# LayerNorm statistics summed over feature tiles on VectorE before the ones-matmul, and a cast moved to ScalarE

## The reference

```python
x = x + cumsum_1024(layernorm(x) @ W.T + bias)        # cumsum along the 1024 features
h = silu(ln(x) @ w1.T * s1) * (ln(x) @ w2.T * s2)     # 1024 -> 4096
h = gelu(h @ h1.T * sh1)                              # 4096 -> 4096
h = gelu(h @ h2.T * sh2)                              # 4096 -> 4096
x = x + (h @ w3.T * s3)                               # 4096 -> 1024
```

## Time and profile before

| | us |
|---|---|
| runs of the kernel before | 2634.89 and 2745.08, median 2689.98 |
| the profiled execution, its own time | 2631.85 |
| its span on the slowest core (core 1) | 2630.3 |
| spans of the 8 cores | 2620.1 to 2630.3 |
| TensorE busy in the span | 2546.2 (97%) |
| VectorE busy | 212.3 (8%) |
| ScalarE busy | 286.9 (11%) |

### The profile page before, as it was taken

The page is one execution under the profiler, slowest core; times in us unless marked ns, Lnnn a source line. Parts: engine busy times, 40 slices in busy tenths (PEclk is TensorE's granted clock), DMA queues, the critical chain, the costliest instruction groups (busy, mean ns, idle before and its releaser), DMA issues.

```text
span 2630.3 us, 25489 instructions; the slowest of 8 cores (2620.1 to 2630.3 us)
## 1 busy us (share of the span) xinstructions
PE 2546.2 (97%) x11708; PEld 1146.1 (44%) x11708; DVE 212.3 (8%) x222; ACT 286.9 (11%) x258; POOL 273.1 (10%) x184
## 2 busy tenths in 40 slices
PE   4899999999999999999968999999999999999999
PEld 1344444444444444444423444444444444444444
DVE  3511100000000000000045111000000000000000
ACT  3311100000000000000032111100000000000000
POOL 0000111111111111111000001111111111111110
PEclk9999999999999999999979999999999999999999
DMA  7265698888888888888752547988988898889873
GB/s 130 34 90 70 68 86 76 76 79 79 74 74 78 80 74 75 77 80 93 109 115 32 84 64 77 92 76 77 80 76 74 76 80 77 73 75 80 80 95 66
DMA packets 635434, 207.30 MB, mean 79 GB/s; under 512 B 594368, under 2 KB 631232, under 8 KB 635328
## 3 DMA queue, kind: packets, MB, share of 16 engines
q0 software_dynamic: 629568, 188.76, 75.2%
q1 hardware_dynamic: 5760, 16.92, 1.9%
HBM read 386.02 MB, written 8.39 MB: 150 GB/s over the span
## 4 chain that ended last, share of the span: by engine, by line
PE 94%; DMA 3%; DVE 2%; ACT 0%; SPq 0%; issue 0%; DVEq 0%; ACTq 0%; POOLq 0%
PE ps L193 94%; DMA x_sb<-xT 2%; DMA wb<-h1T 1%; DVE u_sb L269 1%; DMA outT<-x_sb 0%; PE ps L378 0%; PE ps L389 0%; DVE stat L360 0%; DVE stat L255 0%; SPq L314 0%; DVE stat L275 0%; ACT v_sb L367 0%; SPq L202 0%; DVE v_sb L261 0%; DVE x_sb L534 0%
## 5 line engine op out<-in xcount | busy, mean ns | idle before, releaser
L193 PE MATMUL ps<-v_sb,wb 128*128 128x512 bf16 x6144 | 1330.5, 380 | 12.9 <-DVE v_sb L294 12.9
L193 PE MATMUL ps<-u_sb,wb 128*128 128x512 bf16 x5376 | 1165.3, 379 | 5.4 <-DMA wb<-h1T 5.4
L193 PEld LDWEIGHTS ps<-v_sb,wb 128*128 128x128 bf16 x6144 | 601.9, 98 | 741.2 <-issue 18.6
L193 PEld LDWEIGHTS ps<-u_sb,wb 128*128 128x128 bf16 x5376 | 526.3, 98 | 641.6 <-issue 8.8
L153 POOL DMA_DIRECT2D wb<-h1T x64 | 107.2, 1676 | 784.5 <-PE ps L193 767.6
L153 POOL DMA_DIRECT2D wb<-h2T x64 | 107.2, 1675 | 776.8 <-PE ps L193 776.8
L534 DVE SCALAR_TENSOR_TENSOR x_sb<-ps,s_sb,x_sb 128x1024 f32<-128x1024 f32 x16 | 20.5, 1283 | 1976.0 <-PE ps L193 1976.0
L514 ACT ACTIVATE u_sb<-ps,sh_sb 128x1024 bf16<-128x1024 f32 x64 | 71.3, 1114 | 812.7 <-PE ps L193 812.7
L494 ACT ACTIVATE v_sb<-ps,sh_sb 128x1024 bf16<-128x1024 f32 x64 | 71.3, 1114 | 791.9 <-PE ps L193 791.9
L469 DVE SCALAR_TENSOR_TENSOR u_sb<-ps,s_sb,v_sb 128x1024 bf16<-128x1024 f32 x64 | 82.1, 1284 | 358.8 <-PE ps L193 358.8
L462 ACT ACTIVATE v_sb<-ps,s_sb 128x1024 bf16<-128x1024 f32 x64 | 71.3, 1114 | 356.7 <-PE ps L193 356.7
(11 more groups left out here) (27 smaller groups left out, 110.8 us busy)
## 6 DMA issues: line engine op xcount, KB each, us to landing
wb<-h1T POOLq DMA_DIRECT2D x64, 1024.0 KB, 13.7
wb<-h2T POOLq DMA_DIRECT2D x64, 1024.0 KB, 13.6
wb<-w1T POOLq DMA_DIRECT2D x16, 1024.0 KB, 11.5
wb<-w2T POOLq DMA_DIRECT2D x16, 1024.0 KB, 16.4
wb<-w3T POOLq DMA_DIRECT2D x16, 1024.0 KB, 10.9
x_sb<-xT SPq DMA_DIRECT2D x16, 512.0 KB, 18.2
outT<-x_sb SPq DMA_DIRECT2D x16, 512.0 KB, 3.8
wb<-wT POOLq DMA_DIRECT2D x4, 1024.0 KB, 12.4
```

The costliest lines, as they stand in the source:

```text
L193: return e.matmul(out, lhs, rhs, start=st, stop=sp)
```

## The change

It alters three things.

- **Statistics.** Instead of 8 tiles, groups S and SS now sum two operands each: one tile that VectorE has accumulated over feature tiles 0 to 6 in bfloat16, and tile 7. A group has 4 matmuls where it had 16. The accumulators are tiles 1 (`ACCS`) and 2 (`ACCSS`) of region `XN`. Each is built by a copy for tile 0 and an addition for tiles 1 to 6, all on VectorE.
- **First layernorm.** The addition for a tile's cast is added to VectorE's list right behind that cast; those for the squares are added after all eight casts, ahead of `ev_m`.
- **Attention loop.** The bfloat16 cast of the new x moves from VectorE (L416) to ScalarE, as an Identity activation ahead of the Square, and both additions for tile o are added to VectorE's list behind the running sum of step o, ahead of the product (L360) of step o + 2. They wait for ScalarE's Identity and Square of the same tile.

```diff
+        def emit_acc_add(acc_tile, src_tile, i, waits):
+            if i == 0:
+                def f(e, a=acc_tile, s=src_tile):
+                    return e.tensor_copy(vre(XN, a), s)
+            else:
+                def f(e, a=acc_tile, s=src_tile):
+                    return e.tensor_add(vre(XN, a), vre(XN, a), s)
+            return plan.add("vector", f, waits=waits, inc=s_ve)
 ...
                     xbf_evt[i] = plan.add("vector", fc,
                                           waits=x_ready(i) + [war_xbf_x2], inc=s_ve)
+                    if i < ND - 1:
+                        aS_evt = emit_acc_add(ACCS, vre(XBF, i), i,
+                                              [xbf_evt[i], war_xn, aS_evt])
                 for i in range(ND):
 ...
                     x2_evt[i] = plan.add("scalar", fs,
                                          waits=x_ready(i) + [war_xbf_x2], inc=s_sc)
+                    if i < ND - 1:
+                        aSS_evt = emit_acc_add(ACCSS, vre(X2, i), i,
+                                               [x2_evt[i], war_xn, aSS_evt])
 ...
+            def stats_group(k, acc_tile, tile7_h, a_evt, t7_evt, free_evt):
+                last = None
+                for hh in range(2):
+                    w1_ = [free_evt, consts_evt, a_evt] if hh == 0 else []
+                    def fa(e, k=k, hh=hh, a=acc_tile):
+                        return e.matmul(ps[k][:, hh * 512:(hh + 1) * 512],
+                                        ones_sb[:, 0:P],
+                                        v_sb[:, XN + a * C + hh * 512: XN + a * C + (hh + 1) * 512],
+                                        start=True, stop=False)
+                    plan.add("tensor", fa, waits=w1_)
+                    w2_ = [t7_evt] if hh == 0 else []
+                    def fb(e, k=k, hh=hh, t=tile7_h):
+                        return e.matmul(ps[k][:, hh * 512:(hh + 1) * 512],
+                                        ones_sb[:, 0:P], t(hh),
+                                        start=False, stop=True)
 ...
             kS, freeS = psum_acquire(pool)
-            evS = mm_group(kS, [ones_sb[:, 0:P]] * ND,
-                           lambda i, h: vre_h(XBF, i, h),
-                           first_waits=[freeS, consts_evt],
-                           per_i_waits=lambda i: [xbf_evt[i]])
+            evS = stats_group(kS, ACCS, lambda hh: vre_h(XBF, ND - 1, hh),
+                              aS_evt, xbf_evt[ND - 1], freeS)
             kSS, freeSS = psum_acquire(pool)
-            evSS = mm_group(kSS, [ones_sb[:, 0:P]] * ND,
-                            lambda i, h: vre_h(X2, i, h),
-                            first_waits=[freeSS, consts_evt],
-                            per_i_waits=lambda i: [x2_evt[i]])
+            evSS = stats_group(kSS, ACCSS, lambda hh: vre_h(X2, ND - 1, hh),
+                               aSS_evt, x2_evt[ND - 1], freeSS)
 ...
                 def fc2(e, o=o):
-                    return e.tensor_copy(vre(XBF, o), x_t(o))
-                xbf2_evt[o] = plan.add("vector", fc2, waits=[xadd_evt[o]],
-                                       inc=s_ve)
+                    return e.activation(vre(XBF, o), x_t(o), AF.Identity)
+                xbf2_evt[o] = plan.add("scalar", fc2, waits=[xadd_evt[o]],
+                                       inc=s_sc)
 ...
+                if o < ND - 1:
+                    accS_state[0] = emit_acc_add(
+                        ACCS, vre(XBF, o), o,
+                        [xbf2_evt[o], accS_state[0]] +
+                        ([w1w2_end_pe] if (o == 0 and w1w2_end_pe) else []))
+                    accSS_state[0] = emit_acc_add(
+                        ACCSS, vre(X2, o), o,
+                        [x22_evt[o], accSS_state[0]] +
+                        ([w1w2_end_pe] if (o == 0 and w1w2_end_pe) else []))
```

More of the change, by code:

```diff
@@ L219, in build_nc @@
         stat_r = stat[:, 2 * C:3 * C]
+        ACCS, ACCSS = 1, 2
+        def emit_acc_add(acc_tile, src_tile, i, waits):
[6 more added lines that the diff above has]
+            return plan.add("vector", f, waits=waits, inc=s_ve)
         def ln_phase(x_ready, war_xbf_x2, war_xn, war_tmp, war_ha,
@@ L223, in ln_phase @@
             if precast is not None:
-                xbf_evt, x2_evt = precast
+                xbf_evt, x2_evt, aS_evt, aSS_evt = precast
             else:
@@ L227, in ln_phase @@
                 x2_evt = [None] * ND
+                aS_evt = aSS_evt = None
                 for i in range(ND):
@@ L237, in ln_phase @@
                                          waits=x_ready(i) + [war_xbf_x2], inc=s_sc)
+                    if i < ND - 1:
[16 more added lines that the diff above has]
+                                        start=False, stop=True)
+                    if hh == 1:
+                        last = plan.add("tensor", fb, waits=w2_, inc=s_pe)
+                    else:
+                        plan.add("tensor", fb, waits=w2_)
+                return last
             kS, freeS = psum_acquire(pool)
-            evS = mm_group(kS, [ones_sb[:, 0:P]] * ND,
-                           lambda i, h: vre_h(XBF, i, h),
-                           first_waits=[freeS, consts_evt],
-                           per_i_waits=lambda i: [xbf_evt[i]])
+            evS = stats_group(kS, ACCS, lambda hh: vre_h(XBF, ND - 1, hh),
+                              aS_evt, xbf_evt[ND - 1], freeS)
             kSS, freeSS = psum_acquire(pool)
-            evSS = mm_group(kSS, [ones_sb[:, 0:P]] * ND,
-                            lambda i, h: vre_h(X2, i, h),
-                            first_waits=[freeSS, consts_evt],
-                            per_i_waits=lambda i: [x2_evt[i]])
+            evSS = stats_group(kSS, ACCSS, lambda hh: vre_h(X2, ND - 1, hh),
+                               aSS_evt, x2_evt[ND - 1], freeSS)
             m_ap, msq_ap, r_ap = stat_m, stat_msq, stat_r
@@ L340, in build_nc @@
             sbf_state = [None]
+            accS_state = [None]
+            accSS_state = [None]
             def emit_attn(o):
@@ L434, in build_nc @@
                                      war_tmp=attn_end_pe, war_ha=attn_end_pe,
-                                     precast=(xbf2_evt, x22_evt))
+                                     precast=(xbf2_evt, x22_evt,
+                                              accS_state[0], accSS_state[0]))
             u_evt = [None] * NH
```

## The result

The changed kernel takes 2661.23 us (median of 18 runs, 2650.67 to 3000.19) beside 2640.56 us for the kernel before (17 runs, 2632.10 to 3151.75). The ratio is 1.0082, interval 1.0062 to 1.0102: slower by 0.8%, small but outside the noise. The profiled execution took 2655.36 us. A few executions of either kernel, in which one half of the chip ran slower, make the long upper ends; the ratio leaves them out.

The account below looks back on a forecast made before the run. TensorE, busy 97% of the span, was taken to bound the kernel, except around the layernorms and loop ends. Terms 3.7 + 6.2 + 4.1 + 6.2 = 20.2 us on 2631.85 gave 2652, range 2644 to 2664, wider 2638 to 2712.

Parts of the forecast that it names:

- First layernorm: Each chunk's first layernorm: squares' additions ahead of the mean delay it, +3.7 us, or +4.1 us in the second chunk.
- The term for the wT matmuls: First layernorm: the 32 wT matmuls, now starting after idling, cost nothing; upper bound 3.3 us late at half clock.
- Chained additions: VectorE, first layernorm: an addition waiting for its predecessor takes 0.79 us; 0.60 apart if dependence were not felt.
- Loop: Attention loop: step of 5.19 us instead of 4.32, +0.87 us, set by a loop over VectorE and ScalarE.
- End of the loop: Second layernorm's mean, after the loop's longer steps and its end, starts at 93.1 instead of 86.83: +6.2 us.
- The sign given for this stage: End of the attention loop: from step 7's addition to x (L398) to the mean, 2.5 us.
- rival B: Attention loop: idling lowers TensorE's clock, 20 matmuls take 8.6 us, 41 us more, 2693; chance 0.05.
- The window that was to speak against it: First layernorm: granted clock stayed 1.00 after 1.89 us of TensorE idling before 53.77, cited against a clock drop.
- A: Attention loop: accumulations hide in VectorE's 0.76 us idle per step; only first layernorms cost, 7.8 us, 2640; chance 0.08.
- C: Statistics groups: 96 fewer matmuls at 0.216 us pay in full, 20.7 us, giving 2611; chance 0.04.
- The sum: Both chunks' layernorms and loops: 3.7 + 6.2 + 4.1 + 6.2 = 20.2 us on 2631.85, giving 2652; chance 0.74.
- The range: Whole kernel: own range 2644 to 2664; wider range, leaving out C and little else, 2638 to 2712.

Follow-up runs that it names:

- the halved transfers: Kernel before and changed kernel, each with half of every h1 and h2 weight transfer left out: 2629.4 and 2649.86 us.
- run with the loop alone: Kernel before with only the changed attention loop and second layernorm, first layernorm as before: ratio 1.0055.

## Why the prediction was right and where it was wrong

- **First layernorm**: +3.7 us forecast, 3.69 measured, in both chunks. In the second, the last cast was to be 0.4 late: on the profiled core it was about 0.2, on the eight 0.1 to 0.5. The term for the wT matmuls was rightly put at nothing.
- **Chained additions**: 0.79 forecast, 0.80 measured (4.67 us for six). The Trainium skill, VectorE: DVE Perf Modes, § The DRAIN you can't avoid, says of eight copies that a semaphore after each cost nothing extra. Here an addition that waits for the one before it starts 0.20 us later than an independent instruction does (eight differences in 4.90 us, 0.60 apart). The page does not say whether its copies waited for one another.
- **Loop**: step 5.19 forecast, 5.22 measured, set by the loop over VectorE and ScalarE as worked out. ScalarE's Identity took 1.06 us, as assumed.
- **End of the loop**: mis-sized. First to second mean was to grow by 6.2 us and grew by 7.06. Half of the miss is the alternating order of the four matmuls: I counted two behind tile 7's cast, there are three, at half clock; the run with the other order gave back 0.42. The rest is 0.03 us a step and one step of 5.44, whose cause is open. The sign given for this stage, 2.5 us from L398 of step 7 to the mean, holds only from the addition's end; it was 2.9 there, and 4.12 from its start.
- **Clock** (rival B): 1.00 in the loop with 0.9 us of idling a step, so B is refuted. The window that was to speak against it, 47 to 54, ends 0.23 us after the idling and could not show what follows it (from 53.80 to 60.00 the trace has 1.00 too). The warning cited there (the Trainium skill, TensorE: Matmul & The Clock Gate, § Why this matters for your kernels) is of longer gaps than these, so the page and the trace do not differ. The clock fell at the loop's end (0.74 from 80 to 94), where its price is the matmul just named.
- **Rivals A and C**: A is refuted by the step of 5.22. Its idea is sound, though: with the additions one step later the step is 4.32. C, 20.7 us less for the 96 matmuls, is refuted by the first layernorm, which has 24 matmuls fewer and a mean 3.7 us later, and by the time.
- **The step from the sum to a time is the one that failed.** The sum, 20.2 us, is what was measured: 20.5 us with the weight waits gone, and 0.82%, 22 us, between the whole kernels. But I set it on the profiled execution's 2631.85 and left it there. This execution was at the low end for the kernel before: the median of 17 runs is 2640.56. So 2652 was 9 us too low. And beside the median shown, 2689.98, the middle of 2634.89 and 2745.08, 2652 reads as a gain of 1.4%, the opposite of my own working, while the kernel became 0.8% slower. I said how far the two lay apart and did not say which of them the kernel's time was. The term behind it is TensorE's waits for weights. I took them as they were in that one execution ("so they shift with it"), 5.4 us on its slowest core, and never asked what they are in the others; the halved transfers show that they make about 10 us of the kernel's median.
- **The range**: 2661 lies in the first one, 2644 to 2664, only by its share for the spread between cores; the terms alone end at 2660. The upper end of the wider one, 2712, came from that median and not from a bound of the kernel.
- **The chance of 0.91 for "within 2%"** said less than the trace allowed: all terms had one sign, each known within 1 us, and a 0.8% loss is measurable with enough runs.

## What to carry to other kernels

Taking work off the busiest engine gains nothing where its neighbours' chain sets the end; look at the list in which the replacement will stand, and at what is queued behind it. Work that waits for another engine belongs one step later in an in-order list, or where that engine idles: in the loops of both chunks the same accumulations cost 13 us here and 2 us one step later (both by the stages), and in w3, where VectorE idles, they held nothing up. And a level is not a difference: a sum of stages gives the difference well, while the level needs more than one execution.

## What the runs showed of the hardware

- Over eight cores and over kernels the untouched stages of the first chunk repeat within 0.12 us, while TensorE's waits for weights, 0 to 36 us a core at the same code (run with the loop alone), move the slowest core. With half of each h1 and h2 transfer all these waits are gone. The time to x's last tile varies too, by 3 to 5 us a chunk.
- The second chunk's loop starts at either of two paces: L360 of step 0 to L398 of step 1 took 7.9 us on three cores before and 9.2 to 9.6 on five, 8.2 on six cores after and 9.6 on two. In the median this gave back 1.2 us of the loss. Before, the three cores at 7.9 us had a clock of 1.00 from 1355 to 1370 and the other five 0.89 to 0.93, so the pace seems to follow how much of the first wT matmuls runs at half clock; this was not tried apart.
